# Two graph-attention layers on one core: node groups placed between the last sums, shorter last blocks, skip products at other slots

## The chip, the cores and the metric

One core of a Trainium2 chip runs the whole program. The metric is device time in microseconds (us), from the first to the last instruction with what lies around them. The engines are PE (TensorE), DVE (VectorE), ACT (ScalarE), POOL (GpSimd) and SP (which here only starts DMAs). Each runs its own queue in order, and the queues meet through semaphores.

## What is computed

3125 nodes with 128 features, 50000 edges sorted by destination, two layers of attention with two heads, a residual and a layer norm:

```python
def _transformer_conv(x, src, dst, qw, qb, kw, kb, vw, vb, sw, sb):
    q = (x @ qw + qb).reshape(N, H, D); k = ...; v = ...
    alpha = jnp.einsum('ehd,ehd->eh', q[dst], k[src]) * scale
    m = jax.ops.segment_max(alpha, dst, num_segments=N)
    ex = jnp.exp(alpha - m[dst])
    denom = jax.ops.segment_sum(ex, dst, num_segments=N)
    w = ex / (denom[dst] + 1e-16)
    agg = jax.ops.segment_sum(w[:, :, None] * v[src], dst, num_segments=N)
    return agg.mean(axis=1) + x @ sw + sb
h = _transformer_conv(x, src, dst, q1_w, ...) + x @ lin1_w + lin1_b
out = _transformer_conv(h, src, dst, q2_w, ...) + h @ lin2_w + lin2_b
x = _layernorm(x + out)
```

## The kernel before

**Chunks and bins.** The sorted edges are cut into chunks of 128, with a step for each pair of chunk and bin of 128 nodes: 416 steps (`STEPS`) for 391 chunks and 25 bins. I call a step, too, a chunk. The steps are grouped in blocks (`SIZES`); a block is what one scan of maxima covers.

**A layer.** For each step POOL gathers the 128 source rows by an indirect DMA (L407) into one of 98 ring places of `gathered`. PE spreads q k^T of the destination bin to the edges (`step_t`, L667, three products), and DVE multiplies it with the gathered rows and adds up (`step_alpha`, L930), which gives alpha. When a block has its alphas, `scan` runs over nine slots: PE transposes (L688 to L709), ACT copies (L477 to L485), and DVE does the segmented maxima both ways (L971 to L1010). Then each chunk of the block is weighed: DVE (`far_apart`, L941) or ACT (L492) marks which edge belongs to which node, ACT makes exp of it (`weigh`, L508, one for each head), PE multiplies with the gathered rows into a PSUM bank (`step_u`, L679), and DVE adds the bank to the bin's sums (`step_add`, L961). Three banks take turns.

**The order.** It is written by hand. `slots()` gives for each slot t the step whose alpha is made, the piece of a scan, and the chunks that are weighed; all four engines walk the same list. The chunks of a block are spread evenly over the slots of the next block, from nine slots after its end (`S_SLOTS`); the last block has `TAIL_SLOTS` = 24 slots. In slots without a step of alpha DVE makes all the marks, in the others every sixth (`DVE_EVERY`).

**The end of a layer.** Within the tail, every third slot from slot 421 on, PE makes a group of skip products x @ (s + lin) (`make_skip`, L655) into bank 0 or 1, and DVE copies it into `skip` (L950, layer 0) or adds it to `x_rows` (L953, layer 1). After the last sum come seven node groups of up to four bins (G = 4, the last has one bin). Group g: DVE normalises the sums (`normalise`, L1072 to L1074), PE transposes them (L747, L751), ACT copies ratio and head 0 (L541, L542), and head 1 is copied by DVE in layer 0 (L1086) and by ACT in layer 1 (L544). PE projects with v's weights (bias L762, products L767) into `bank_p`, of which there are two. DVE adds the skip rows (L1095 or L1100). In layer 0 PE transposes the result (L778), ACT copies it into `xT` (L549), and SP stores it to `h_d` (L356), from which layer 1 gathers; POOL waits for all seven stores (L400). In layer 1 DVE makes the statistics (L1105 to L1116), ACT the root (L553) and the normalised rows (L558), and SP stores them (L362, L366).

On each engine the loop over g does, in one turn, the newest step of group g and the later steps of groups g-1, g-2 and g-3. Here is the order of one turn on PE: transposes of group g; projection of group g-1; in layer 0 the transposes of group g-2's result.

## Time and profile before

| | before |
|---|---|
| median of three runs | 1239.3 us (1238.72 to 1239.43) |
| span of the profiled execution | 1238.0 us |
| PE busy | 993.4 us, 80% |
| DVE busy | 983.5 us, 79% |
| ACT busy | 784.5 us, 63% |
| POOL busy | 801.5 us, 65% |
| mean granted PE clock | 0.940 of 2.4 GHz |

The busy shares are means over stages that differ. POOL is busy at one level through both layers and idle between them and at the end, as the slices of the page show. So the two stretches after the last gather of a layer are read apart from the rest. In the rows of a timeline the columns are start, duration, engine, line, operation, out<-in, count, and in brackets the idle time before it with what ended it. PEld is PE's weight load, which starts a product.

### The profile page before, as it was taken

Reading aid. Unit: us, or ns where it says so; the run is one execution under the profiler, and the core shown is the slowest. Engines: PE = TensorE matmul, PEld = TensorE weight load, DVE = VectorE, ACT = ScalarE, POOL = GpSimd, SP = SyncE. Lnnn points to the kernel's source line nnn. Section 1 sums busy time; section 2 is a strip of 40 time slices with the busy share of each in tenths; the row PEclk is TensorE's granted clock in tenths of the full one; section 3 lists DMA queues with packets and bytes.
Section 4 is the critical chain, followed back from the end, with each engine's and each line's share of the span. In section 5 each row is a group of like instructions: output and inputs, shape, how many; then the busy total and the mean of one; then the engine's idle time right before and its main releaser. Section 6 shows DMA issues by size and latency. Waiting matters only on the chain.

```text
span 1238.0 us, 30556 instructions
## 1 busy us (share of the span) xinstructions
PE 993.4 (80%) x6796; PEld 791.4 (64%) x6796; DVE 983.5 (79%) x5252; ACT 784.5 (63%) x2594; POOL 801.5 (65%) x854
## 2 busy tenths in 40 slices
PE   4868987878877878789896776978886878888887
PEld 2647766766666667678653655757675757667775
DVE  4799986878787878889567687878787887879876
ACT  0456866676676768677254564758575768678655
POOL 3777777777777777750057777777777777777100
PEclk9989999899999999999797999999899999999888
DMA  4223332222222222210032222222232323222001
GB/s 112 88 77 89 89 84 80 78 80 80 78 81 80 78 82 84 73 42 1 27 102 79 79 80 77 80 80 78 80 87 71 89 73 85 77 80 63 17 2 52
DMA packets 53531, 90.21 MB, mean 73 GB/s; under 512 B 17499, under 2 KB 25969, under 8 KB 53361
## 3 DMA queue, kind: packets, MB, share of 16 engines
q0 software_dynamic: 26624, 54.58, 16.4%
q1 hardware_dynamic: 24145, 32.62, 8.7%
q8 instruction: 67, 1.10, 0.4%
q10 hardware_dynamic: 2592, 1.07, 0.3%
q14 instruction: 103, 0.84, 0.2%
HBM read 84.86 MB, written 3.34 MB: 71 GB/s over the span
## 4 chain that ended last, share of the span: by engine, by line
DMA 28%; PE 21%; POOL 20%; issue 15%; DVE 13%; ACT 2%; DVEq 1%; SPq 0%; POOLq 0%; ACTq 0%
POOL gathered L407 20%; DMA gathered<-h_rows,src_e 14%; DMA gathered<-in_x,src_e 14%; PE ps L679 9%; PE ps L667 5%; DVE acc L961 4%; DVE junk L930 3%; PE ps L767 2%; PE ps L751 1%; PE ps L762 1%; ACT whot L508 1%; DVE max_b L999 1%; DVE apart L941 1%; DVE max_f L997 1%; PE ps L655 0%
## 5 line engine op out<-in xcount | busy, mean ns | idle before, releaser
L508 ACT ACTIVATE whot<-apart,below 128x128 f32<-128x128 bf16 x1664 | 550.3, 388 | 139.7 <-DVE apart L941 127.5
L679 PE MATMUL ps<-gathered,whot 128*128 128x129 f32 x3328 | 566.1, 297 | 62.4 <-ACT whot L508 44.0
L930 DVE SCALAR_TENSOR_TENSOR junk<-ps,gathered 128x129 f32<-128x129 f32 x1664 | 413.0, 286 | 163.6 <-issue 113.8
L667 PE MATMUL ps<-table,hot_t 128*128 x2496 | 445.7, 287 | 101.8 <-DVE junk L930 80.5
L679 PEld LDWEIGHTS ps<-gathered,whot 128*128 128x128 f32 x3328 | 457.1, 200 | 100.0 <-DVE acc L961 64.7
L407 POOL DMA_INDIRECT gathered<-in_x,src_e x416 | 399.8, 961 | 144.3 <-issue 68.0
L407 POOL DMA_INDIRECT gathered<-h_rows,src_e x416 | 397.5, 955 | 126.6 <-issue 62.2
L667 PEld LDWEIGHTS ps<-table,hot_t 128*128 128x128 bf16 x2496 | 249.3, 100 | 212.3 <-issue 157.3
L961 DVE TENSOR_TENSOR acc<-ps,acc 128x258 f32 x832 | 350.2, 421 | 14.9 <-PE ps L679 5.4
L492 ACT ACTIVATE apart<-col_b,ndl_e 128x128 bf16<-128x128 bf16 x618 | 239.2, 387 | 0.0
L930 DVE DVE_READ_ACCUMULATOR junk<-ps,gathered 128x1 f32 x1664 | 134.9, 81 | 0.4
L477 ACT COPY a_row<-ps 48x256 f32<-48x256 f32 (+5 forms) x20 | 7.3, 365 | 89.2 <-PE ps L688 89.2
L941 DVE TENSOR_SCALAR apart<-ncol_b,ndl_e 128x128 bf16<-128x128 bf16 x214 | 54.9, 256 | 0.0
L400 POOL MEMSET gathered<- 128x98 f32 x1 | 0.3, 271 | 80.0 <-DMA h_rows<-table 80.0
L920 DVE TENSOR_SCALAR hot_t<-dl_bc,part_f 128x1024 bf16<-128x1024 bf16 x104 | 51.7, 497 | 0.1
L481 ACT ACTIVATE shrink<-drop 2x1 f32<-2x1 f32 x20 | 4.0, 202 | 52.9 <-DVE drop L988 52.9
L485 ACT COPY below<-ps 128x96 f32<-128x96 f32 (+5 forms) x20 | 4.6, 228 | 52.1 <-PE ps L709 52.1
L644 PE MATMUL ps<-qk,xT 128*128 128x258 f32 x100 | 33.7, 423 | 0.6 <-ACT xT L549 0.6
L767 PEld LDWEIGHTS ps<-wv,gathered 128*128 128x128 f32 x200 | 26.6, 214 | 10.8 <-issue 10.6
L471 ACT CAST table<-left 128x258 bf16<-128x258 f32 x50 | 20.4, 408 | 15.0 <-DVE left L865 13.3
L767 PE MATMUL ps<-wv,gathered 128*128 128x128 f32 x200 | 29.5, 306 | 0.0
L865 DVE TENSOR_TENSOR left<-ps,table 128x258 f32<-128x258 f32 x50 | 21.0, 421 | 8.0 <-ACT table L468 4.3
(165 smaller groups left out, 561.0 us busy)
## 6 DMA issues: line engine op xcount, KB each, us to landing
dl_bc<-local_dst_rows SPq DMA_DIRECT2D x104, 256.0 KB
gathered<-in_x,src_e POOLq DMA_INDIRECT x416
gathered<-h_rows,src_e POOLq DMA_INDIRECT x416
h_rows<-table SPq DMA_DIRECT2D x6, 256.0 KB, 2.3
out<-x_rows SPq DMA_DIRECT2D x6, 256.0 KB
table<-in_L_gnn_q_w ACTq DMA_DIRECT2D x2, 128.0 KB
table<-in_L_gnn_k_w ACTq DMA_DIRECT2D x2, 128.0 KB
wv<-in_L_gnn_v_w ACTq DMA_DIRECT2D x2, 128.0 KB
```

The source lines that it names most:

```text
L407: nc.gpsimd.indirect_dma_start(out=gathered[:, t % RING, 0:F], out_offset=None, in_=rows[:, :], in_offset=bass.IndirectOffsetOnAxis(ap=src ...
L492: nc.scalar.activation(apart[:, c % UN, :], col_b[:, :], ACT.Square, bias=ndl_e[:, c:c + 1]).then_inc(S["apart_act"], 1)
L508: last = nc.scalar.activation(whot[:, c % UN, h, :], apart[:, c % UN, :], ACT.Exp, scale=FAR, bias=below[:, j % 2, h, o:o + 1])
L644: nc.tensor.matmul(bank_u[n % NB][:, 0:CW], xT[:, k * P:(k + 1) * P], qk[:, l, :], start=True, stop=False)
L667: last = nc.tensor.matmul(bank_t[n % NB][:, 0:CW], hot_t[:, n // BC % 2, t % BC, :], table[:, bass.ds(b, 1), part, :].rearrange("p o c -> ...
L679: last = nc.tensor.matmul(bank_u[n % NB][:, h * C1:(h + 1) * C1], whot[:, c % UN, h, :], gathered[:, c % RING, :], start=True, stop=True)
L767: last = nc.tensor.matmul(o, uT[q % 2][:, h, t * P:(t + 1) * P], wv[:, l, h * F:(h + 1) * F], start=False, stop=(t == k - 1 and h == HEADS ...
L865: V.tensor_tensor(left[:, n % 2, :], bank_u[n % NB][:, 0:CW], table[:, k, 0, :], ALU.subtract).then_inc(S["left_ready"], 1)
L920: V.tensor_scalar(hot_t[:, q % 2, :, :].rearrange("p k e -> p (k e)"), dl_bc[:, q % 2, :], part_f[:, 0:1], None, ALU.is_equal).then_inc(S[ ...
L930: last = V.scalar_tensor_tensor(out=junk[:, t % 2, h, :], in0=bank_t[n % NB][:, h * C1:(h + 1) * C1], scalar=1.0, in1=gathered[:, t % RING ...
L941: V.tensor_scalar(apart[:, c % UN, :], ncol_b[:, :], ndl_e[:, c:c + 1], None, ALU.not_equal).then_inc(S["apart_dve"], 1)
L961: V.tensor_tensor(bin_acc, bank_u[n % NB][:, 0:CW], bin_acc, ALU.add).then_inc(S["u_added"], 1)
```

## The change

Sizes of the blocks are 26, 36, 44, five of 48, then 42, 18 and 10: eleven blocks, not ten. The last block has 10 slots. There are 435 slots instead of 449, and then five more for the node groups. The node groups are placed by `norm_at`: group g is normalised in the first slot by which its last sum is added, slot 424 at the earliest, one group a slot; `node(l, g)` follows in the next. This gives normalise at slots 424, 425, 426, 427, 429, 433, 435 and node(0 to 6) at 425, 426, 427, 428, 430, 434, 436. Chunks 406 to 415 are weighed in slots 425 to 434, one a slot. The sums use two banks from chunk 388 on (`TWO_BANKS`), and the projection has one bank, bank 6, which is also that of the scans' rows and of the skip products. A skip group is made at slot 12 after the end of blocks 1 to 7. Its product goes in layer 0 into `x_rows` in the place of x, so x is loaded again in layer 1. The stores of h stand on SP's queue behind the first two loads of `dl_bc` of layer 1.

```diff
-SIZES = (26, 36, 44) + 4 * (48,) + (44, 40, 34)
+SIZES = (26, 36, 44) + 5 * (48,) + (42, 18, 10)
+TWO_BANKS = STARTS[-3]
-TAIL_SLOTS = 24
+TAIL_SLOTS = SIZES[-1]
-SKIP_SLOT, SKIP_EVERY = 5, 3
+SKIP_BLOCK, SKIP_SLOT = 1, 3
+SPARE = 24, 72
...
-        skip = tmp([BINS, F])
...
-        tmp = lender(gathered[:, :, :].rearrange("p s c -> p (s c)"))
+        tmp = lender(gathered[:, SPARE[0]:SPARE[1], :].rearrange("p s c -> p (s c)"))
...
-        bank_p = [ps[:, 3, :], ps[:, 4, :]]
+        bank_p = ps[:, 6, :]
...
+        def u_bank(c):
+            return bank_u[c % NB] if c < TWO_BANKS else bank_u[c % 2]
         def skip_group(t, late):
-            g, rest = divmod(t - STEPS - SKIP_SLOT - late, SKIP_EVERY)
-            return g if rest == 0 and 0 <= g < NGR else None
+            for g in range(NGR):
+                if t == STARTS[SKIP_BLOCK + g + 1] + S_SLOTS + SKIP_SLOT + late:
+                    return g
+            return None
+        def last_step(g):
+            return min(CHUNKS - 1 + G * g + G - 1, STEPS - 1)
...
+            norm_at[g] = max(added_at[last_step(g)], STEPS + S_SLOTS - 1, norm_at[g - 1] + 1 if g else 0)
+        NODE_SLOTS = range(LAST_SLOT + 1, norm_at[NGR - 1] + 5)
+        def node_tick(t):
+            return [g for g in range(NGR) if norm_at[g] == t - 1] + [g for g in range(NGR, NGR + 3)
+                                                                     if norm_at[NGR - 1] + g - NGR + 2 == t]
...
@@ SP: as before, and @@
+            def store_h():
+                for g in range(NGR):
+                    t0, k, _ = group(g)
+                    sp.wait_ge(S["rows_read"], g + 1)
+                    sp.dma_start(h_d.rearrange("(t p) f -> p t f", p=P)[:, t0:t0 + k, :],
+                                 h_out[g % 2][:, 0:k, :]).then_inc(h_saved[g % 2], 16)
+                load_x(S["x_again"])
...
+                    if l == 1 and q == 2:
+                        store_h()
...
@@ ACT, PE: the body of the old loop over g is now node(l, g), and @@
+                    for g in node_tick(t):
+                        node(l, g)
+                for t in NODE_SLOTS:
+                    for g in node_tick(t):
+                        node(l, g)
...
@@ PE, make_skip @@
-                pe.wait_ge(S["alpha_ready"], (l + 1) * STEPS)
-                if g >= 2:
-                    pe.wait_ge(S["skip_read"], l * NGR + g - 1)
+                pe.wait_ge(S["below_ready"], l * NBLK + SKIP_BLOCK + g + 1)
...
@@ PE, step_u @@
-                if n >= NB:
-                    pe.wait_ge(S["u_added"], n - NB + 1)
+                if c in (TWO_BANKS, TWO_BANKS + 1):
+                    pe.wait_ge(S["u_added"], n)
+                elif c > TWO_BANKS:
+                    pe.wait_ge(S["u_added"], n - 1)
+                elif n >= NB:
+                    pe.wait_ge(S["u_added"], n - NB + 1 if c >= NB else n)
...
@@ PE, scan, piece 0 @@
+                    if j > SKIP_BLOCK:
+                        pe.wait_ge(S["skip_read"], l * NGR + min(j - SKIP_BLOCK, NGR))
...
@@ PE, node, before the projection of q = g - 1 @@
-                        if q >= 2:
-                            pe.wait_ge(S["rows_read"], m - 1)
+                    if q >= 1:
+                        pe.wait_ge(S["rows_read"], m)
...
@@ DVE, read_skip @@
-                    V.tensor_copy(skip[:, t0:t0 + k, :], product).then_inc(S["skip_read"], 1)
+                    V.tensor_copy(rows, product).then_inc(S["skip_read"], 1)
                 else:
-                    rows = x_rows[:, t0:t0 + k, :]
+                    if g == 0:
+                        dve.wait_ge(S["x_again"], 32)
                     V.tensor_tensor(rows, rows, product, ALU.add).then_inc(S["skip_read"], 1)
...
@@ DVE, normalise, and the loop @@
+                dve.wait_ge(S["u_added"], l * STEPS + last_step(g) + 1)
+                if g == 0:
+                    dve.wait_ge(S["skip_read"], (l + 1) * NGR)
...
+                    for g in range(NGR):
+                        if norm_at[g] == t:
+                            normalise(l, g)
+                    for g in node_tick(t):
+                        node(l, g)
                 step_add(l, STEPS - 1, b[UN - 1])
```

`node(l, g)` on DVE does, in this order: in layer 0 the copy of head 1 of group g; then the add of the skip rows of group g-2, which frees `bank_p`; in layer 1 that group's statistics and the reciprocal root of group g-3. On ACT: the copies of group g; in layer 0 the copy of group g-2's result into `xT`; in layer 1 the root of group g-2 and the normalised rows of group g-3.

## Rows read from the trace of the kernel before

**Rows 1.** Waits: engine, line, released by, us in total, times, longest.
```profile
POOL gathered L400 <- DMA h_rows<-table: 80.0, 1, 80.0
```
**Rows 2.** Timeline, the end of the gathers of layer 0 and the last alpha.
```profile
547.77 0.94 POOL L407 DMA_INDIRECT gathered<-in_x,src_e  x1 [0.30 <-issue]
...
551.39 0.29 DVE L930 SCALAR_TENSOR_TENSOR junk<-ps,gathered 128x129 f32<-128x129 f32 x1 [0.67 <-issue]
```
**Rows 3.** Timeline, DVE, first and tenth alpha of the slots of block 8's scan.
```profile
509.10 0.28 DVE L930 SCALAR_TENSOR_TENSOR junk<-ps,gathered 128x129 f32<-128x129 f32 x1
...
523.32 0.28 DVE L930 SCALAR_TENSOR_TENSOR junk<-ps,gathered 128x129 f32<-128x129 f32 x1
```
**Rows 4.** Windows, L679 alone: stretch, length, busy (count) of PE and PEld, clock, DMA.
```profile
525.08:551.39 26.31, 17.95 (x110) 14.09 (x108) 1.00 0.20 51
```
**Rows 5.** Timeline, the tail of layer 0 and the first two normalises.
```profile
565.86 0.48 DVE L1021 TENSOR_SCALAR acc<-acc,factor  x2
...
581.07 7.84 ACT L508 ACTIVATE whot<-apart,below 128x128 f32<-128x128 bf16 x26 [0.35 <-DVE apart L941]
...
581.90 7.83 PE L679 MATMUL ps<-gathered,whot 128*128 128x129 f32 x52
...
584.57 0.43 DVE L961 TENSOR_TENSOR acc<-ps,acc 128x258 f32 x1
584.91 0.24 DVE L941 TENSOR_SCALAR apart<-ncol_b,ndl_e 128x128 bf16<-128x128 bf16 x1
...
590.41 0.17 DVE L1072 TENSOR_SCALAR gathered<-acc 128x8 f32<-128x8 f32 x1
...
592.00 0.16 DVE L1072 TENSOR_SCALAR gathered<-acc 128x8 f32<-128x8 f32 x1
```
**Rows 6.** Timeline, a group of skip products and its copy.
```profile
568.81 1.06 PE L655 MATMUL ps<-wskip,xT 128*128 128x128 f32 x8
...
570.00 0.68 DVE L950 COPY table<-ps 128x512 f32<-128x512 f32 x1
```
**Rows 7.** Timeline, one turn of the node groups of layer 0.
```profile
612.68 0.09 PEld L747 LDWEIGHTS ps<-ident,gathered 128*8 128x8 f32 x1
...
613.86 0.29 PEld L762 LDWEIGHTS ps<-bias_rows,ratio 10*128 10x128 f32 x2 [0.17 <-issue]
...
613.97 0.69 DVE L1086 COPY gathered<-ps 128x512 f32<-128x512 f32 x1 [1.58 <-PE ps L751]
...
614.58 0.68 DVE L1095 TENSOR_TENSOR table<-table,ps 128x512 f32<-128x512 f32 x1
...
614.91 2.05 PE L767 MATMUL ps<-wv,gathered 128*128 128x128 f32 x16
...
617.13 0.09 PEld L747 LDWEIGHTS ps<-ident,gathered 128*8 128x8 f32 x1
...
617.44 0.58 ACT L549 COPY xT<-ps 128x512 f32<-128x512 f32 x1 [2.74 <-PE ps L778]
```
**Rows 8.** Timeline, POOL's restart for layer 1.
```profile
628.67 0.27 POOL L400 MEMSET gathered<- 128x98 f32 x1 [79.95 <-DMA h_rows<-table]
```
**Rows 9.** Timeline, layer 1: last gather, first normalise, a projection, the last rows.
```profile
1152.03 0.94 POOL L407 DMA_INDIRECT gathered<-h_rows,src_e  x1 [0.30 <-issue]
...
1194.61 0.17 DVE L1072 TENSOR_SCALAR gathered<-acc 128x8 f32<-128x8 f32 x1
...
1217.48 0.29 PEld L762 LDWEIGHTS ps<-bias_rows,ratio 10*128 10x128 f32 x2 [0.17 <-DVE x_rows L1100]
...
1230.40 0.28 DVE L1100 TENSOR_TENSOR x_rows<-x_rows,ps 128x128 f32<-128x128 f32 x1
```
**Rows 10.** Timeline, ACT before the first root.
```profile
1210.78 1.28 ACT L553 ACT_TABLE_LOAD   x1
```
**Rows 11.** Windows (columns: PE, PEld, DVE, ACT, POOL, clock) and a projection soon after.
```profile
592.00:596.00 4.00, 2.89 (x14) 2.55 (x15) 3.18 (x8) 0.73 (x2) 0.00 (x0) 0.50 0.00 0
...
599.20 3.78 PE L767 MATMUL ps<-wv,gathered 128*128 128x128 f32 x16
```

More of the change, by code:

```diff
@@ L782, in _ @@
+                    for g in node_tick(t):
+                        node(l, g)
+                for t in NODE_SLOTS:
+                    for g in node_tick(t):
+                        node(l, g)
         @block.vector
```

289 lines of the change are left out of this document (149 added, 140 removed).

## The prediction

> **What bounds the kernel now.** I read the waits first, then the timeline at the two ends of the gathers, then the stretches between. POOL issues one gather each 1.25 us (0.94 busy, 0.30 issue) [rows 2], 416 a layer, and nothing moves it from that pace: that is the bound of the steady part. Then it stands still for 80.0 us, until the last rows of h have landed [rows 1]. So a layer is a paced part, in which other engines have slack, and a part after the last gather (547.77, its sums' last step of alpha at 551.39 [rows 2]), in which PE, DVE and ACT set the time. That second part runs to POOL's restart at 628.67 [rows 8] and, in layer 1, from 1152.03 to the end [rows 9]. It has two pieces: the remaining sums, until the first normalise at 590.41 [rows 5] and 1194.61 [rows 9], and the node groups. Only a change of these pieces, twice, can move the span. I sum against the profiled span of 1238.0 us; the median run is 1239.3, so 1.3 is added at the end.
>
> **Prices.** PE: 52 products of sums in 7.83 us, so 0.60 a chunk [rows 5]. ACT: 26 weights in 7.84, so 0.30 an activation; a chunk costs two, and a third where ACT makes apart [rows 5]. DVE: a sum and the next apart start 0.34 apart, apart adds 0.24: 0.58 a chunk in the tail [rows 5]. Between 525.08 and 551.39 the schedule has 28 chunks and 23 steps of alpha (the row holds 110 products, 55 a head [rows 4]): 28 x 0.60 leaves 9.5, 0.41 of PE a step. PE was full there. A scan with its nine steps and ten chunks took 509.10 to 523.32, 14.2 us [rows 3]; DVE's own work there is 9 x 0.42 + 10 x 0.34 + about 6.4 of scan + 0.7, so DVE sets a scan stretch.
>
> **Skip products moved.** A group is 1.06 us of PE and 0.68 of DVE [rows 6]. Seven leave the tail of each layer. In the steady part a block of 48 slots lasts 60 us and needs about 49 of PE and 48 of DVE; 1 us more is caught up before the gathers end, so I cost it at nothing there (if the cover were gone: 7 us a layer). The waits it adds (PE for below_ready at slot 12 after a block, the next scan for skip_read) are for work done slots before.
>
> **x loaded twice.** On SP's queue it stands behind the h stores and ahead of the loads of dl_bc from the third on. Its reader is DVE at slot 75, some 90 us later. Zero; the upper bound is one late dl_bc, a few us, which the ring would absorb. The h stores now stand behind two loads of dl_bc whose buffers were free long before: zero.
>
> **Blocks.** Sizes 5 x 48, 42, 18, 10 for 4 x 48, 44, 40, 34. After the last step of alpha 27 chunks remain instead of 45, but the list of slots shows the price: slots 397 to 414 carry 42 chunks, 2.33 each, and one more scan is in them. Stage by stage, from slot 388 at 509.10 + 6 x 1.25 = 516.6 (gather pace):
> Slots 388 to 396, a scan with 11 chunks: 14.2 [rows 3], to 530.8.
> Slots 397 to 405, 21 chunks: ACT 60 activations x 0.30 = 17.9, PE 9 x 0.41 + 21 x 0.60 = 16.3, DVE 12. With handovers 18.4, to 549.2; the gathers would have allowed 11.3.
> Slots 406 to 414, 21 chunks and a scan: ACT 18.4, DVE 14.2 + 11 x 0.34 = 17.9, PE 17.3. Three full queues, 19, to 568.2.
> Slots 415 to 424: before, nine such slots with 11 chunks and two skip copies took 14.0 (551.8 to the rescale at 565.86 [rows 5]). Seven more chunks on DVE (+4.1), no skip copies (-1.2), one alpha (+0.4): 17.3, to 585.5.
> Two PSUM banks for the sums from chunk 388 on let a chunk pass in about 0.67 instead of 0.60: hidden by DVE here. So at 585.5 ten chunks are left and all skips are done; before, at that time, some nine chunks were left. The blocks gain next to nothing: the work was moved into slots that were full too. All gain must come from the node groups beginning 4.9 us earlier.
>
> **Node groups between the sums, layer 0.** PE's work from there is 10 x 0.60 + 6.25 groups x 4.45 (612.68 to 617.13 [rows 7]) = 33.8. But the queues run in order, and I followed them group by group:
> One bank_p. PE's projection of group g-1 now waits until DVE has read group g-2, and DVE reads it only behind its copy of group g's transposes. In the trace the copy begins at 613.97, the read at 614.58 for 0.68, while PE went on at 613.86 [rows 7]. So PE stands 1.35 us in each of five groups: 6.8.
> ACT's place. node(g) on ACT ends with the wait for h_tp and the copy of xT (0.58 [rows 7]); the weights of the next chunk stand behind it, and PE's chunk behind those: from the end of h's transposes to PE's next product 1.4, three times: 4.2.
> Start: normalise(0) 1.6 (590.41 to 592.00 [rows 5]) and the copies that transposes(1) needs: 1.7 + 1.8. Normalise(5), which waits for the sum of chunk 413: 1.5. Last groups' handovers 0.9. Store to restart 1.6.
> Sum 52.3: restart at 637.8, not 628.67: **+9.1**.
>
> **Layer 1.** The first normalise comes 36.8 after the last gather's issue, at 1189.8. PE: 6.0 + 6.25 x 4.0 = 31.0. Here ACT makes both copies and one bank_p costs little: at 1217.48 PE already goes on as DVE's read ends [rows 9]. What it meets instead is the root. Now one table load stands before the first root, 1.28 us [rows 10], and the exponentials are over by then. With roots at slots 427, 428, 430 and 434 and exponentials between them, ACT must load seven times instead of once. By my walk through the queues PE waits 1.8, 3.5 and 3.6 us for the weights of chunks 409, 410 and 412, behind copies, root, two loads and four normalised tiles. With start 3.0, normalise(5) 1.3, handovers 2.5 and the 7.6 from the last rows' add (1230.40) to the end [rows 9]: 31.0 + 8.9 + 14.4 = 54.3, end at 1244.1: **+6.1**.
> The page "ScalarE: Activation LUTs" of the Trainium skill (Table sets: the hidden batching unit) speaks against this: do all of one set, then the other, since exp then sqrt means two loads. By its 2.66 us a switch, drain included, six more would cost some 8 us more than the sum has; in the trace the root follows the load directly, so I keep 1.28.
>
> **Clock.** From 592 to 605 PE was granted 0.50, that is 1.2 GHz [rows 11], after it had stood while the first group was normalised; sixteen projections took 3.78 against 2.05 at 2.4 GHz [rows 11, 7]. That loss, about 5.5 us a layer, is in the time before. After the change no single long gap stands there, but PE is idle over 1 us twice a group. Bounds: nothing, or half speed for most of the phase (+3.3 a group). I take half of what was lost before, 2.7 a layer: +5.4.
> The page "TensorE: Matmul & The Clock Gate" (A second HAM failure mode: psum-queue depth-cycling) of the Trainium skill describes such short gaps between groups as making the clock swing; it is the clock rival below, and no stretch before has just this pattern.
>
> **Sum.** 1238.0 + 9.1 + 6.1 + 5.4 + 1.3 = 1259.9; I say 1259.
>
> **Rivals.**
> It works as meant (faster): PE stays filled, since chunks and groups cover each other's waits. Restart at 585.5 + 33.8 + 1.7 + 1.6 = 622.6, end 7.9 earlier by the same sum: 1225. For it: 38.3 us of node phase now hold 28 of PE work. It decides if PE's gap behind a group's transposes is under 0.3 us. Against: the copy stands first on DVE. 0.08.
> No change: the projection and ACT waits fall into each other, 11 us of them go: about 1240. 0.06.
> Root and exponential share a table after all: 6 x 1.28 less, 5 of them on the path: 1253. Against: the load before the first root. 0.08.
> The clock stays at 1.2 GHz for most of both node phases: 20 more, 1279. For it: PE's new gaps come in every group, where the one gap before was enough [rows 11]. 0.15.
> The forecast, own range 1250 to 1270: 0.63.
>
> **How the numbers follow.** The measurement tells about 0.2% from no change. Faster 0.09, within it 0.05, slower 0.86. From 1240 to 1279 leaves out the faster case, part of the even one and half of the clock's: 0.18. The largest unknown inside is the first normalise (580 to 590).
>
> **What would show it.** The last step of alpha comes near 568 instead of 551 with the gathers' end unchanged; the first normalise at 585 +- 4; PE waiting for DVE's add of rows 1.3 us a group in layer 0; seven table loads in the tail of layer 1 (eight in all, with the one at the start); skip products in the steady part without a later gather. I am wrong if alpha ends before 560, or if the node groups take under 45 us from the first normalise in layer 0.

## The result, and the profile after

| | before | after |
|---|---|---|
| median of four runs | 1239.01 us (1236.45 to 1239.43) | 1282.97 us (1279.99 to 1285.69) |
| ratio, 95% interval | | 1.036 [1.034, 1.038] |
| span of the profiled execution | 1238.0 us | 1281.6 us |
| mean granted PE clock | 0.940 | 0.917 |

The change makes the kernel 44 us slower, where 20 were forecast: the direction holds, the size doesn't. First the waits of the changed kernel (engine, line, released by, us in total, times, longest; L435 is POOL's restart, L723 the sums' products, L543 their weights, L1016 DVE's add, L563 the copy of `xT`, L785 the projection's bias, L1114 the add of the skip rows):

```profile
POOL gathered L435 <- DMA h_rows<-table: 101.3, 1, 101.3
...
PE ps L723 <- ACT whot L543: 63.2, 71, 3.4
...
DVE acc L1016 <- PE ps L723: 49.1, 50, 7.0
...
ACT xT L563 <- PE ps L801: 27.4, 7, 5.8
...
PE ps L785 <- DVE table L1114: 6.5, 5, 1.4
```

POOL stands 101.3 us where it stood 80.0 [rows 1]: 21.3 of the 43.6 us between the spans lie in this pause between the gathers of the two layers. Then the timeline, at the places of [rows 2, 5, 8, 9]:

```profile
517.40 0.29 DVE L983 SCALAR_TENSOR_TENSOR junk<-ps,gathered 128x129 f32<-128x129 f32 x1
...
548.07 0.95 POOL L442 DMA_INDIRECT gathered<-in_x,src_e  x1 [0.30 <-PE ps L723]
...
550.02 0.28 DVE L983 SCALAR_TENSOR_TENSOR junk<-ps,gathered 128x129 f32<-128x129 f32 x1
...
572.79 0.28 DVE L983 SCALAR_TENSOR_TENSOR junk<-ps,gathered 128x129 f32<-128x129 f32 x1
...
594.27 0.17 DVE L1092 TENSOR_SCALAR gathered<-acc 128x8 f32<-128x8 f32 x1
...
650.28 0.27 POOL L435 MEMSET gathered<- 128x98 f32 x1 [101.26 <-DMA h_rows<-table]
...
1175.49 0.95 POOL L442 DMA_INDIRECT gathered<-h_rows,src_e  x1 [0.30 <-issue]
...
1220.93 0.16 DVE L1092 TENSOR_SCALAR gathered<-acc 128x8 f32<-128x8 f32 x1
```

The steps of alpha are those of slots 388, 406 and 415. The last gather of layer 0 ends 0.3 us later. The first normalise comes at 594.27, 3.9 us *later* than before, though 27 chunks and not 45 were left behind the last alpha and ten of them stand behind it; and from there to the restart it is 56.0 us, where it was 38.3. In layer 1 the gathers take 524.9 us from first to last, against 523.0; the first normalise comes 44.5 us after the last gather's end, against 41.6; from it to the end it is 60.7, against 43.4.

What PE waits for in the node groups of layer 0:

```profile
606.41 1.12 PE L785 MATMUL ps<-bias_rows,ratio 10*128 10x512 f32 x2 [1.38 <-DVE table L1114]
...
611.31 0.68 PE L723 MATMUL ps<-gathered,whot 128*128 128x129 f32 x4 [1.36 <-ACT whot L543]
...
614.35 1.12 PE L785 MATMUL ps<-bias_rows,ratio 10*128 10x512 f32 x2 [1.38 <-DVE table L1114]
...
619.25 1.27 PE L723 MATMUL ps<-gathered,whot 128*128 128x129 f32 x8 [1.36 <-ACT whot L543]
...
622.87 1.12 PE L785 MATMUL ps<-bias_rows,ratio 10*128 10x512 f32 x2 [1.38 <-DVE table L1114]
...
629.40 2.67 PE L723 MATMUL ps<-gathered,whot 128*128 128x129 f32 x16 [1.36 <-ACT whot L543]
...
633.07 0.28 PE L770 MATMUL ps<-ident,gathered 128*8 128x128 f32 x1 [1.00 <-DVE gathered L1094]
...
635.60 1.12 PE L785 MATMUL ps<-bias_rows,ratio 10*128 10x512 f32 x2 [1.38 <-DVE table L1114]
...
642.02 1.12 PE L785 MATMUL ps<-bias_rows,ratio 10*128 10x512 f32 x2 [0.98 <-DVE table L1114]
```

Two waits alternate. PE waits 1.38 us ahead of a projection, because there is only one bank, and 1.36 ahead of a chunk's products, because of the place of the `xT` copy in ACT's queue. In layer 1 there are also the table loads on ACT (first the loads, then PE's waits for weights):

```profile
1253.81 1.28 ACT L567 ACT_TABLE_LOAD   x1
...
1255.11 0.21 ACT L567 ACTIVATE gathered<-gathered 128x4 f32<-128x4 f32 x1
...
1256.87 1.28 ACT L543 ACT_TABLE_LOAD   x1
...
1225.88 1.20 PE L723 MATMUL ps<-gathered,whot 128*128 128x129 f32 x4 [1.99 <-ACT whot L543]
...
1241.25 0.68 PE L723 MATMUL ps<-gathered,whot 128*128 128x129 f32 x4 [1.88 <-ACT whot L543]
...
1250.30 1.27 PE L723 MATMUL ps<-gathered,whot 128*128 128x129 f32 x8 [1.12 <-ACT whot L543]
...
1259.00 3.71 PE L723 MATMUL ps<-gathered,whot 128*128 128x129 f32 x16 [3.42 <-ACT whot L543]
```

The grouped lines count four loads at the root (L567) and three at the exponentials (L543) in this stretch. And this is a hole in the sums at slot 406, the first of the scan of the block of 18 (ACT, then DVE):

```profile
550.93 0.36 ACT L512 COPY a_row<-ps 18x256 f32<-18x256 f32 x1 [1.42 <-PE ps L734]
...
551.20 0.40 ACT L527 ACTIVATE apart<-col_b,ndl_e 128x128 bf16<-128x128 bf16 x1
...
551.51 0.68 ACT L543 ACTIVATE whot<-apart,below 128x128 f32<-128x128 bf16 x2
...
550.56 0.43 DVE L1016 TENSOR_TENSOR acc<-ps,acc 128x258 f32 x1
...
553.22 0.43 DVE L1016 TENSOR_TENSOR acc<-ps,acc 128x258 f32 x1 [2.24 <-PE ps L723]
```

ACT waits 1.42 us for PE's transposes of the new block's alphas (L734) while the next weights stand behind that copy; the sums then miss 2.24 us.

### The profile page after: what moved, and what is told of

The parts are those of the page before. It is cut to its first block, busy times and chain, and to the rows that moved or that the text cites. A ratio compares the mean times of both kernels' runs of the same rounds, so it can differ in the third digit from the quotient of the medians.

```text
span 1281.6 us, 30697 instructions
## 1 busy us (share of the span) xinstructions
PE 1014.7 (79%) x6824; PEld 809.9 (63%) x6824; DVE 989.4 (77%) x5268; ACT 801.3 (63%) x2636; POOL 804.4 (63%) x854
## 4 chain that ended last, share of the span: by engine, by line
PE 33%; issue 18%; DVE 15%; DMA 14%; POOL 13%; ACT 5%; DVEq 1%; SPq 0%; ACTq 0%; POOLq 0%
PE ps L723 17%; POOL gathered L442 13%; PE ps L707 10%; DMA gathered<-h_rows,src_e 7%; DMA gathered<-in_x,src_e 6%; DVE junk L983 5%; DVE acc L1016 4%; ACT whot L543 3%; PE ps L790 2%; PE ps L774 1%; DVE max_b L1054 1%; PE ps L785 1%; DVE max_f L1052 1%; PE ps L695 1%; DVE a_end L1026 1%
## 5 line engine op out<-in xcount | busy, mean ns | idle before, releaser
L723 PE MATMUL ps<-gathered,whot 128*128 128x129 f32 x3328 | 583.0, 304 | 79.6 <-ACT whot L543 63.2
L543 ACT ACTIVATE whot<-apart,below 128x128 f32<-128x128 bf16 x1664 | 553.7, 388 | 142.0 <-DVE apart L994 126.3
L723 PEld LDWEIGHTS ps<-gathered,whot 128*128 128x128 f32 x3328 | 472.7, 206 | 123.4 <-DVE acc L1016 70.8
L707 PE MATMUL ps<-table,hot_t 128*128 x2496 | 452.3, 291 | 107.6 <-DVE junk L983 86.3
L1016 DVE TENSOR_TENSOR acc<-ps,acc 128x258 f32 x832 | 349.9, 421 | 59.3 <-PE ps L723 49.1
L707 PEld LDWEIGHTS ps<-table,hot_t 128*128 128x128 bf16 x2496 | 253.2, 102 | 211.8 <-issue 157.3
L527 ACT ACTIVATE apart<-col_b,ndl_e 128x128 bf16<-128x128 bf16 x648 | 250.8, 387 | 0.0
L512 ACT COPY a_row<-ps 48x256 f32<-48x256 f32 (+6 forms) x22 | 8.0, 365 | 97.7 <-PE ps L734 97.7
L435 POOL MEMSET gathered<- 128x98 f32 x1 | 0.3, 273 | 101.3 <-DMA h_rows<-table 101.3
L994 DVE TENSOR_SCALAR apart<-ncol_b,ndl_e 128x128 bf16<-128x128 bf16 x184 | 46.4, 252 | 0.0
L516 ACT ACTIVATE shrink<-drop 2x1 f32<-2x1 f32 x22 | 4.5, 202 | 56.1 <-DVE drop L1043 56.1
L520 ACT COPY below<-ps 128x96 f32<-128x96 f32 (+6 forms) x22 | 4.9, 223 | 47.7 <-PE ps L755 47.5
L790 PE MATMUL ps<-wv,gathered 128*128 128x128 f32 x200 | 32.6, 327 | 0.0
L506 ACT CAST table<-left 128x258 bf16<-128x258 f32 x50 | 20.4, 407 | 16.4 <-DVE left L918 14.7
```

The source lines that it names most:

```text
L527: nc.scalar.activation(apart[:, c % UN, :], col_b[:, :], ACT.Square, bias=ndl_e[:, c:c + 1]).then_inc(S["apart_act"], 1)
L543: last = nc.scalar.activation(whot[:, c % UN, h, :], apart[:, c % UN, :], ACT.Exp, scale=FAR, bias=below[:, j % 2, h, o:o + 1])
L707: last = nc.tensor.matmul(bank_t[n % NB][:, 0:CW], hot_t[:, n // BC % 2, t % BC, :], table[:, bass.ds(b, 1), part, :].rearrange("p o c -> ...
L723: last = nc.tensor.matmul(u_bank(c)[:, h * C1:(h + 1) * C1], whot[:, c % UN, h, :], gathered[:, c % RING, :], start=True, stop=True)
L790: last = nc.tensor.matmul(o, uT[q % 2][:, h, t * P:(t + 1) * P], wv[:, l, h * F:(h + 1) * F], start=False, stop=(t == k - 1 and h == HEADS ...
L994: V.tensor_scalar(apart[:, c % UN, :], ncol_b[:, :], ndl_e[:, c:c + 1], None, ALU.not_equal).then_inc(S["apart_dve"], 1)
```

## The experiments

Five sets of two to four kernels, each beside the kernel before on its chip. **The chips differ**: in the first set the kernel before took 1237.6 us, as in the result; in the others, on four other chips, 1647.5, 1624.1, 1646.2 and 1640.3. So a kernel is compared with those of its own set, and between sets only by ratio. The ratios are the record's and can differ by 0.003 from the ratio of the two medians. One more view helps: how long a layer runs after its last gather is issued, split at the start of the reciprocal of the first normalise (the second instruction of that step). In layer 0 it ends with the first gather of layer 1, in layer 1 with the program. It is read from one profiled execution of each kernel:

| kernel, set | layer 0: to normalise, to restart | layer 1: to normalise, to end |
|---|---|---|
| before | 42.8, 38.4 | 42.8, 43.2 |
| after | 46.4, 56.1 | 45.6, 60.5 |
| e2_skip, 1 | 39.6, 37.2 | 39.1, 41.9 |
| e10_blocks_skip, 1 | 51.1, 37.2 | 48.7, 42.3 |
| e7_old_blocks, 1 | 28.2, 75.7 | 28.0, 79.3 |
| e3_rows_first, 1 | 48.6, 44.9 | 47.2, 60.3 |
| e4_three_banks, 2 | 86.8, 61.1 | 86.8, 62.3 |
| e5_roots_last, 2 | 89.2, 62.3 | 90.4, 50.9 |
| e6_xt_later, 2 | 92.3, 51.5 | 90.4, 64.2 |
| e8_all_fixed, 2 | 89.5, 46.0 | 89.3, 50.9 |
| after_again, 3 | 91.5, 56.3 | 91.3, 59.4 |
| e12_four_edits, 3 | 85.1, 48.0 | 87.8, 51.6 |
| e12_again, 4 | 88.2, 43.7 | 86.2, 48.4 |
| e10_again, 4 | 93.9, 37.2 | 94.2, 41.9 |
| e11_again, 4 | 92.1, 37.2 | 90.5, 42.3 |
| e13_five, 5 | 83.4, 43.7 | 83.8, 49.8 |
| e11_third, 5 | 91.2, 37.2 | 90.5, 43.5 |

### Set 1: the parts one by one

**e2_skip**: old blocks, node groups at the end with two projection banks, three sum banks throughout. Only the skip products, the second load of x and the place of the h stores are new. Against the changed kernel (the lines that carry the edit; `...` stands for lines left out):

```diff
-SIZES = (26, 36, 44) + 5 * (48,) + (42, 18, 10)
+SIZES = (26, 36, 44) + 4 * (48,) + (44, 40, 34)
-TWO_BANKS = STARTS[-3]
+TWO_BANKS = STEPS
-TAIL_SLOTS = SIZES[-1]
+TAIL_SLOTS = 24
...
-        bank_p = ps[:, 6, :]
+        bank_p = [ps[:, 3, :], ps[:, 4, :]]
...
-            norm_at[g] = max(added_at[last_step(g)], STEPS + S_SLOTS - 1, norm_at[g - 1] + 1 if g else 0)
+            norm_at[g] = LAST_SLOT + 1 + g
...
```

> The changed kernel with the old blocks (44, 40, 34, tail of 24 slots), all node groups behind the last sum, three banks for the sums and two for the projection: of the change only the skip products in the steady part, x loaded twice and the later place of the h stores are left. Theory (the skips are covered there): seven groups of 1.06 us of PE leave each tail, about 5 us a layer come back, less 2 us for a slower start of layer 1's gathers: 1239 - 8 = about 1231. Rival (the steady part has no room, each group delays alphas up to the end): 1239 or more.

1232.5 us (1231.4 to 1233.7), ratio 0.996 [0.994, 0.998]: below before by 0.4%, which is small but outside the interval, and 1.5 us above the 1231 of the theory. **e10_blocks_skip** is the same kernel with the new sizes.

> The same as the kernel with the skips moved alone, but with the new blocks (48, 42, 18, 10): the difference of the two is the blocks. In the changed kernel the first normalise came at 594.3 with ten chunks (6.7 us) left, so the last sum would be at 601, against about 585 with old blocks. Theory (slots 397 to 424 are full and one more scan stands in them): 10 to 16 us a layer more than the skips alone, 1251 to 1262. Rival (as my prediction had it, the blocks only move work, +-1 us a layer): within 3 us of the skips alone.

1254.1 us (1251.6 to 1256.4), ratio 1.013 [1.011, 1.016]. So the blocks alone cost 21.6 us, about half in each layer, as the theory had it; the forecast had them at nothing. In the table the time to the first normalise goes from 39.6 to 51.1 and from 39.1 to 48.7, and the node groups stay as they were. The time lies in the 18 slots ahead of the last alpha, which now carry 42 chunks.

**e7_old_blocks**: the changed kernel with the old sizes; node groups between the sums of a last block of 34 chunks.

```diff
-SIZES = (26, 36, 44) + 5 * (48,) + (42, 18, 10)
+SIZES = (26, 36, 44) + 4 * (48,) + (44, 40, 34)
-TAIL_SLOTS = SIZES[-1]
+TAIL_SLOTS = 24
```

> The changed kernel with the old blocks; the node groups still stand between the last sums (the first in the slot of chunk 394's sum). Together with the three others this closes a table of two by two. Theory (blocks and the placing of the groups both cost, and add up): 1283 less twice 10 to 16, 1250 to 1262; so 20 to 25 us more than the skips alone. Rival (placing the groups costs only in the crowded slots of the new blocks): below 1240.

1285.4 us (1283.0 to 1285.9), ratio 1.038 [1.036, 1.040]. All that was expected is missed: I had priced the interleaving as the same whatever the blocks. With the old blocks it costs 53 us (1285.4 against 1232.5), with the new 29 (1283.0 against 1254.1), perhaps because 22 chunks and not ten then stand among the groups, each with its waits; that was not tested. And the old sizes move something else with them: `TWO_BANKS = STARTS[-3]` is then chunk 342 and no longer 388, so the sums have two banks for 74 chunks of a layer and not for 28. How much of the 53 is that, no run tells. The two parts of the change don't add.

**e3_rows_first**: in layer 0 DVE adds the rows of group g-2 and only then makes the copy of group g's transposes; six lines change place.

```diff
             def node(l, g):
-                if l == 0 and g < NGR:
-                    ... V.tensor_copy(uT[g % 2][:, 1, 0:w], bank_h1[:, 0:w]).then_inc(S["uT1_ready"], 1)
                 if 2 <= g < NGR + 2:
                     ...
+                if l == 0 and g < NGR:
+                    ... V.tensor_copy(uT[g % 2][:, 1, 0:w], bank_h1[:, 0:w]).then_inc(S["uT1_ready"], 1)
```

> The changed kernel with one edit on DVE: in layer 0 the add that reads the projection's bank stands ahead of the copy of the next group's transposes. Theory (PE waits 1.35 us a group for that add, because of the one bank): five groups, 1283 - 6.8 = 1276, all of it in layer 0 between the first normalise and the restart of the gathers (56.0 to about 49). Rival (the wait for ACT's copies or for the weights ends last anyway): less than 2 us.

1275.4 us (1270.1 to 1278.2), ratio 1.030 [1.026, 1.033], 7.6 us less than the changed kernel of the result. In layer 0 the wait of the bias for DVE's add goes from 6.5 us to 0.3; the other 1.2 stood in layer 1 already and stay:

```profile
PE ps L785 <- DVE x_rows L1113: 1.2, 2, 0.8
...
PE ps L785 <- DVE table L1108: 0.3, 1, 0.3
```

```profile
611.65 0.68 PE L723 MATMUL ps<-gathered,whot 128*128 128x129 f32 x4 [1.36 <-ACT whot L543]
...
618.14 1.27 PE L723 MATMUL ps<-gathered,whot 128*128 128x129 f32 x8 [1.35 <-ACT whot L543]
...
625.22 2.68 PE L723 MATMUL ps<-gathered,whot 128*128 128x129 f32 x16 [1.35 <-ACT whot L543]
```

The 1.36 of ACT stand untouched. The cause of the term "one bank_p, 6.8" is shown. The 7.6 us aren't its size alone: by the table layer 0's node groups take 11.2 us less, and 2.2 and 1.6 come back ahead of the first normalises. Of the 11.2, PE's idle time is 5.8 and its busy time 5.5, for it was granted the full clock here and 0.88 in the changed kernel (window from the first normalise to the restart; length, then PE, PEld, DVE, ACT, POOL busy, clock, DMA):

```profile
596.10:641.10 45.00, 35.50 (x237) 27.31 (x238) 24.06 (x57) 13.78 (x39) 0.27 (x1) 1.00 0.13 38
```

### Set 2: the other orders, one by one

**e4_three_banks**: chunk 388 is weighed in slot 415, so the changed kernel has two banks from slot 415 on, and this one from chunk 406, slot 425.

```diff
-TWO_BANKS = STARTS[-3]
+TWO_BANKS = STARTS[-2]
```

> The changed kernel, but the sums keep three banks up to slot 406 + 9 = 415 instead of 406, that is, two banks are used only in the last block. Theory (two banks tie sum and add together: DVE's add waited 5.0 us on PE and PE 4.5 us on DVE's add between 574 and 594 us, against 1.6 and 0.9 in the kernel with the new blocks and the nodes at the end): nothing in slots 406 to 414, where the stage was as long with three banks, and little in the last block, which still has two: 1281 to 1285, a ratio to the kernel before of 1.034 to 1.038. Rival (two banks from 406 on are what made the stage 406 to 414 take 22.8 us and not 19): both layers get back 3 to 4 us: about 1275, 1.030.

**e5_roots_last**: in layer 1 all roots and what follows them from node(6) on.

```diff
-                if l == 1 and 2 <= g < NGR + 2:
-                    t0, k, _ = group(g - 2)
+                for q in late(l, g, 2):      # from g = 6 on, first 0 to 4 at once
+                    t0, k, _ = group(q)
... and so for late(l, g, 3), on ACT the normalised rows, on DVE the reciprocal roots
```

> The changed kernel, but in layer 1 the square roots, reciprocals and normalised rows of the groups begin only at the seventh group step, so that the exponentials of the remaining slots come before all roots and ScalarE changes its table once and not seven times. Theory (each change back costs PE its wait of 1.1 to 3.4 us on the next weights, less 0.7 as usual: 1.9, 2.0, 1.1 and 3.4 us are the four waits): 5 to 8 us less, all in layer 1: 1275 to 1278, a ratio of 1.029 to 1.032. Rival (the loads lie beside matmuls at half clock anyway): 1281 to 1283.

**e6_xt_later**: ACT's copy of h's transposes at the head of the next turn.

```diff
             def node(l, g):
+                if l == 0 and 3 <= g < NGR + 3:
+                    q = g - 3 ...
+                    nc.scalar.copy(xT[:, t0 * P:t0 * P + w], bank_b[:, 0:w]).then_inc(S["hT_ready"], 1)
                 if g < NGR:
                     ...
-                if l == 0 and 2 <= g < NGR + 2:
-                    q = g - 2 ...
-                    nc.scalar.copy(xT[:, t0 * P:t0 * P + w], bank_b[:, 0:w]).then_inc(S["hT_ready"], 1)
```

> The changed kernel, but ScalarE's copy of the transposed h of a group stands one group step later, at its head, when the transposes have long been made. Theory (in layer 0 the weights behind that copy come late and PE waits 1.36 to 1.38 us on them, six times, of which about half would be waited for the node transposes anyway): 4 to 6 us less in layer 0, nothing in layer 1: 1277 to 1279, a ratio of 1.031 to 1.033. Rival (PE's clock and its sequence set the node phase, the wait only moves): 1281 to 1283.

**e8_all_fixed**: e3, e5 and e6 together.

> The changed kernel with three edits together: VectorE adds the projected rows ahead of its copy in layer 0 (7.6 us by a run), roots last (5 to 8) and ScalarE's copy a step later (4 to 6). If they add: 1283 - 7.6 - 6.5 - 5 = 1264, a ratio of 1.020. If what remains is PE's own work at a low clock, the second and third give back little: 1272 to 1275. Either way it stays above the kernel with the new blocks and the nodes at the end (1254): what remains between them is not orders and table loads but work on PE between its sums.

Medians 1692.5, 1691.9, 1692.6 and 1671.2 beside 1647.5; ratios 1.025 [1.022, 1.028], 1.025 [1.022, 1.029], 1.025 [1.022, 1.029] and 1.012 [1.008, 1.016]. The absolute expectations are void on this chip, and the changed kernel itself was not in the set. By its ratios on two other chips, 1.036 and 1.033, each single edit takes off 0.8 to 1.1%; by the medians alone it is 0.3 to 0.9%. Within the set, e8 lies 20.8 us below e5, which lacks rows first and the later copy, and 21.4 below e6, which lacks rows first and the late roots. With 7.6 for rows first, that leaves 13 to 14 for either of the other two. Its 1.012 is below the 1.020 that was expected if the edits add. Whether it stays above the kernel with the new blocks and the nodes at the end is open across chips: that one has 1.013 on the first chip and, in set 4, 1.007.

The traces tell what kind of time it is. PE's idle time, its busy time and its granted clock, from the reciprocal of the first normalise to the restart or to the end:

| kernel | layer 0: idle, busy, clock | layer 1: idle, busy, clock |
|---|---|---|
| after | 15.3, 40.9, 0.88 | 19.7, 40.8, 0.78 |
| after_again | 15.3, 41.0, 0.88 | 19.6, 39.7, 0.81 |
| e3 (rows first) | 9.5, 35.4, 1.00 | 19.2, 41.0, 0.79 |
| e4 (three banks) | 16.6, 44.5, 0.83 | 20.2, 42.1, 0.76 |
| e5 (roots last) | 15.8, 46.4, 0.80 | 16.5, 34.4, 0.86 |
| e6 (copy later) | 12.0, 39.5, 0.90 | 18.7, 45.5, 0.70 |
| e8 (all three) | 5.6, 40.4, 0.85 | 16.5, 34.4, 0.86 |
| e12_four_edits | 6.3, 41.7, 0.82 | 17.2, 34.4, 0.86 |
| e12_again | 6.3, 37.4, 0.92 | 17.2, 31.2, 0.90 |
| e13_five | 6.3, 37.4, 0.92 | 17.2, 32.6, 0.90 |

The idle time hardly changes between traces of the same order. The busy time does: e12 is one kernel, run on two chips, and its layer 0 differs by 4.3 us, all of it busy time at another clock. So a difference of a few us between two single traces isn't yet the edit's.
Roots last: 50.9 us from the first normalise to the end, against 62.3 and 64.2 in the set; 5 to 8 were expected. Over all traces here, the five with the roots last take 48.4 to 51.6 and the five with the roots between 59.4 to 64.2: **about 11 us** between the means. Only 3 of it is idle time (19.7 to 16.5). The rest is PE's busy time: every one of the five with the roots last has a clock of 0.86 to 0.90 there, every one of the others 0.70 to 0.81. One table load is left in that stretch.
Copy later: 51.5 us to the restart, against 61.1 and 62.3 in the set, but against only 56.1 and 56.3 in the two traces of the changed kernel: **5 to 11 us**, where 4 to 6 were expected. The idle time falls by 3.3 to 4.6, which is the forecast's 4.2; the rest goes with a clock of 0.90 against 0.80 to 0.88, and e12 shows that the clock of this stretch moves by 0.10 without an edit. What is left on PE:

```profile
852.32 1.28 PE L723 MATMUL ps<-gathered,whot 128*128 128x129 f32 x8 [0.25 <-DVE acc L1016]
...
854.60 0.28 PE L770 MATMUL ps<-ident,gathered 128*8 128x128 f32 x1 [1.00 <-DVE gathered L1094]
...
857.13 1.83 PE L785 MATMUL ps<-bias_rows,ratio 10*128 10x512 f32 x2 [1.38 <-DVE table L1114]
```

Three banks: 86.8 us to the first normalise in both layers; the six numbers of the kernels of the set without that edit have a mean of 90.2. **About 3.4 us a layer**, and the traces of sets 3 and 4 agree: 85.1 to 88.2 with three banks (e12_four_edits, e12_again), 91.5 and 91.3 without (after_again). The theory said little, the rival 3 to 4: the rival has the size, but not the place. It laid the time on slots 406 to 414, and there the changed kernel has three banks itself. The time lies behind slot 415, where the theory saw no room: from its alpha to the reciprocal in layer 0, e4 takes 18.3 us, e5 20.4 and after_again 22.8.

### Sets 3 to 5: the sum of the edits, and the start of a block

**e12_four_edits** (e8 with three banks) and **after_again** (the changed kernel as it is):

> The changed kernel with four edits together: VectorE's add of the projected rows ahead of its copy in layer 0, ScalarE's copy of the transposed h a group step later, roots and normalised rows of layer 1 only from the seventh group step on, and three sum banks up to the last block. By the traces of the runs with one or three of these edits (time from the last gather to the restart of layer 1, and from the last gather of layer 1 to the end): rows first 7 to 8 in layer 0; copy later 7 to 8 in layer 0; roots last 11 to 13 in layer 1; three banks 3.4 in each layer. If they add on the changed kernel: 1283 - 7.6 - 7.6 - 12 - 6.8 = 1249, a ratio to the kernel before of 1.008. Rival (PE's clock and its longer queue set what remains, orders only move waits): 1262 or more, 1.019.

> The changed kernel once more, unchanged, to stand beside the others of this set on one chip: 1283, a ratio to the kernel before of 1.036. If the three runs with one edit each, all at 1692 beside 1647 for the kernel before, brought nothing, the absolute distance to before is 44 there and here; if they brought what their traces show, this kernel stands further from before on such a chip: about 50 to 55.

1646.9 and 1673.7 beside 1624.1: ratios 1.014 [1.010, 1.017] and 1.033 [1.031, 1.036]. The edits together take 26.8 us off. The sum of the pieces was 34, which would have given 1.008; the rival had 1.019, and the measured value lies between. Either the edits share some of their effect, or the pieces, read from single traces, were taken too large. The changed kernel's distance to before, 49.6, lies just under what was expected from working edits (50 to 55), and 4.5 to 5.2 above that of the three single edits in set 2. **e12_again**, set 4:

> The changed kernel with the four edits (rows first, copy a step later, roots last, three banks up to the last block). On the other chip it was 26.8 us under the changed kernel beside it, where the sum of the single edits by their traces was 34. If the edits add in the same measure here: 1283 - 27 = 1256, a ratio of 1.014; if a chip with faster gathers shows them in full, 1249, 1.008.

1663.7 beside 1646.2, ratio 1.011 [1.009, 1.012], again between the two that were expected. Neither chip was of the first kind, so what the four bring there was not measured.

**e11_blocks_behind** and **b1_skip_behind** are e10 and e2 with one move in ACT's list, the copy of a block's row behind the weights of its slot:

```diff
-                    if s is not None:
+                    if s is not None and s[-1]:
                         scan(l, *s)
                     for c in cs:
                         ...
                         weigh(l, c)
+                    if s is not None and not s[-1]:
+                        scan(l, *s)
```

> The kernel with only the skip products moved, x loaded twice and the stores behind (old blocks, nodes at the end, 1232.5 measured), and in ScalarE's list the copy of a block's row of scores (the first piece of its scan) stands behind the weights of the slot and not ahead of them. Theory (ScalarE stood 1.4 us at that copy on PE's row transposes at each block's first slot while the weights of the slot were ready to be made): 11 blocks a layer, but only where ScalarE is what the sums wait for, in the drain: 0 to 3 us less: about 1231. Rival (the copy then comes later, and with it the maximum, the below row and the block's first weight): 0 to 4 more.

> The kernel with the new blocks, skips moved and the nodes at the end (1254.1 measured), with the same move of ScalarE's row copy behind the weights of its slot. Theory (of the 3.8 us by which slots 406 to 414 took longer than reckoned, the 3.5 us hole in the sums at the first slot of the short block comes from that wait in ScalarE's order): about 2 us less in each layer: 1250, a ratio of 1.010. Rival (the hole is the row transposes and the copy themselves, whatever their order): 1254.

1614.1, ratio 0.993 [0.991, 0.996], and 1628.0, ratio 1.003 [1.001, 1.006], where 0.996 and 1.013 stood for the kernels without the move on the first chip. The first is what the theory had, the second is below its 1.010. Set 4 holds the pair on one chip:

> The kernel with the new blocks, the skips moved and the nodes at the end, unchanged, as the yardstick for the next run on its chip. On a chip of the first set's kind 1254, a ratio of 1.013; on one of the kind of the second and third set the same distance of 16 us to before if the blocks cost the same there, 4 to 6 if the gathers' later landing covers part of what they cost.

> The same kernel with ScalarE's row copy behind the weights of its slot. Theory (ScalarE stood 92 us in all, 22 times, on the row transposes at that copy, 16.9 of it in the last five blocks of layer 0, and the 3.5 us hole in the sums at the first slot of the short block comes from it): 4 to 10 us under the kernel of the run beside it. Rival (the hole only moves): within 1.5 us of it.

> The kernel with only the skips moved, old blocks, nodes at the end, and ScalarE's row copy behind the weights of its slot: without the last edit it took 1232.5, a ratio of 0.9958. Theory: 2 to 6 us less, a ratio of 0.991 to 0.994. Rival: 0.996 or more.

e10_again 1657.3, 1.007 [1.005, 1.010]: 11.1 us above before, neither the 16 nor the 4 to 6. e11_again 1646.8, 1.000 [0.998, 1.002], and b1_again 1633.8, 0.992 [0.991, 0.994], as the theories had them. The move is worth 10.4 us there with the new blocks; with the old ones no pair stands on one chip. How much of it lies after the last gather the timelines tell, first without the move (set 4), then with it (e11_third, set 5):

```profile
763.45 0.43 DVE L1016 TENSOR_TENSOR acc<-ps,acc 128x258 f32 x1
...
766.12 0.43 DVE L1016 TENSOR_TENSOR acc<-ps,acc 128x258 f32 x1 [2.24 <-PE ps L723]
...
763.82 0.36 ACT L512 COPY a_row<-ps 18x256 f32<-18x256 f32 x1 [1.42 <-PE ps L734]
...
786.74 0.36 ACT L512 COPY a_row<-ps 10x256 f32<-10x256 f32 x1 [2.16 <-PE ps L734]
```

```profile
765.12 0.43 DVE L1018 TENSOR_TENSOR acc<-ps,acc 128x258 f32 x1
...
766.12 0.43 DVE L1018 TENSOR_TENSOR acc<-ps,acc 128x258 f32 x1 [0.57 <-PE ps L725]
...
765.73 0.34 ACT L512 COPY a_row<-ps 18x256 f32<-18x256 f32 x1
...
786.75 0.36 ACT L512 COPY a_row<-ps 10x256 f32<-10x256 f32 x1 [0.24 <-PE ps L736]
```

Between two adds 2.67 us become 1.00, and the ten slots from one copy to the next 22.9 become 21.0: 1.9 us. From the alpha of slot 406 to that of slot 415 it is 22.75 without the move and 21.09 in the three traces of e11, which has it. The first two waits of e10_again are the same to the hundredth as in the changed kernel on the first chip (1.42, 2.24), so the slow gathers play no part in them. The table shows more: from the last gather to the first normalise 93.9 and 94.2 become 91.2 to 92.1 and 90.5, that is 5.5 to 6.4 us in the two layers together. The rest of the 10.4 is not placed; the waits at block starts earlier in the layer might carry it, and no run tests that.

**e13_five** (e12 with that move) and **e11_third**:

> The changed kernel with the four edits (rows first, copy a step later, roots last, three banks up to the last block) and also ScalarE's row copy behind the weights of its slot. Theory: that last edit brought 10 us without the steps between the sums (1646.8 beside 1657.3) and brings as much here: a ratio to before of 1.003 to 1.005. If the steps between the sums were worth their overlap once the orders are mended, it would come out under the kernel of the run beside it; what the sets so far say is that it stays 5 to 8 us above it. Rival (with groups between the sums the order at the block's start no longer matters): 1.010.

> The kernel with the new blocks, skips moved, nodes at the end and the row copy behind the weights, beside the run above. On a chip where the gathers land as in the trace of before: 1244 to 1250, a ratio of 1.005 to 1.010, if the edit is worth 2 to 5 us per layer in the drain alone; 1254, 1.013, if the whole of its 10 us lay in waits that slow gathers make. On one where they land later: 1.000.

1645.6 (1635.2 to 1649.3), 1.003 [1.000, 1.006], and 1647.6, 1.004 [1.002, 1.007]. The 1.003 is as expected; the second lies between the values given for the two kinds of chip. With all orders mended the groups between the sums cost nothing more than at the end, and bring nothing. The expected 5 to 8 us between them are missed.

The best kernel of the study is e2's with ACT's move: 0.993 and 0.992 on two chips. Without the move, 0.996 on the first. Both lie below the kernel before by more than their intervals, though by less than 1%, and neither has the blocks or the groups between the sums.

## Why the forecast was wrong

**The sums' end was priced too low: +8.8 us in layer 0, +7.7 in layer 1.** The forecast had the first normalise 36.8 us after the last gather (it says its issue; by its 1189.8 it counts from the end, 0.94 later). Measured are 45.2 and 44.5; in layer 0 the gather itself ends 0.3 later. Stage by stage in layer 0: slot 388 at 517.40 for 516.6 and slot 406 at 550.02 for 549.2, so up to there only 0.8 of start. Then "three full queues, 19" took 22.8, and "17.3, to 585.5" took 21.5.
Slots 406 to 414: the step that failed is the sum of queues' work without the order in them. It took the longest of ACT 18.4, DVE 17.9 and PE 17.3 and 0.6 for handovers, but at the slot where a scan begins ACT waits in order, with the weights behind. Shown: 1.7 to 1.9 of the 3.8 us. The other 2 stay open.
Slots 415 to 424: the step "two banks ... hidden by DVE here" failed; no row stood behind its 0.67 us a chunk either. With the nodes at the end and three banks, e10_blocks_skip took 18.8 from the alpha of slot 415 (573.24) to the rescale (592.02), against 21.5 in the changed kernel, and by e4 a layer gets back about 3.4 us. So 2.7 to 3.4 of the 4.2 us are the two banks, and about 1 stays open. The windows show that the clock falls too (PE, PEld, DVE, ACT, POOL busy, clock, DMA), the changed kernel first, e10_blocks_skip behind it:

```profile
574.00:594.30 20.30, 16.02 (x83) 13.40 (x81) 14.84 (x57) 12.14 (x39) 0.00 (x0) 0.75 0.00 0
```

```profile
574.00:592.00 18.00, 14.11 (x86) 11.77 (x84) 15.81 (x60) 13.21 (x44) 0.00 (x0) 0.91 0.00 0
```

PE was granted 0.75 against 0.91. How much of the 3.4 is the bank itself and how much the clock was not told apart.

**The clock in the node groups: about 5.5 us in layer 0, and more in layer 1, for 2.7 each.** It can be read from PE's busy time. In layer 0 the same PE instructions were busy 35.4 us in e3, at full clock, and 40.9 in the changed kernel, at 0.88. In layer 1 they were busy 40.8 at 0.78, and 31.2 in e12_again at 0.90. Here are the windows of the changed kernel, layer 0 and layer 1:

```profile
594.30:650.30 56.00, 40.93 (x236) 31.85 (x236) 23.87 (x57) 13.62 (x38) 0.02 (x1) 0.89 0.10 30
1221.00:1281.60 60.60, 40.94 (x211) 31.54 (x211) 31.17 (x120) 33.47 (x78) 0.00 (x0) 0.78 0.09 27
```

In e12_again PE was busy for about the 31.0 of the sum, so its work itself was not priced too low there. The rival in which PE stays at 1.2 GHz for most of both phases is out: the means are 0.89 and 0.78 (before: 0.82 and 0.79). But the clock took about 10 us more than the forecast had, half of the rival's 20.

**Node groups of layer 0: the waits right, the total by some luck.** 52.3 and 2.7 for the clock were forecast, 56.0 measured. The waits that the walk through the queues gave, 1.35 in each of five groups and 1.4 three times, are there as 1.38 (four times, and a 0.98) and 1.36 (three times), and the edits took them away: 5.8 and 3.3 us of idle time one by one, 9.7 together, for 6.8 and 4.2 forecast. But the terms as they are listed add up to 53.9 and not to 52.3; the 1.6 from store to restart is missing from the sum. And in the total two misses cancel: PE was idle for 15.3 us where the sum leaves 18.5 beside PE's work, and busy for 40.9 where it has 36.5 with the clock.

**Node groups of layer 1: 3.7 us too low.** 57.0 were forecast, 60.7 measured. Seven loads came as counted, and the PE waits of 1.8, 3.5 and 3.6 as 1.88, 1.12 and 3.42, with one of 1.99 ahead of them. The waits weren't the step that failed: PE was idle for 19.7 us, where the sum has 23.3 beside PE's work. It was busy for 40.8, where 31.0 and 2.7 for the clock stood. So the term that was too small is the clock's, by 7 us. The sixteen products behind the 3.42 took 3.71 us (1259.00), where sixteen in layer 0 took 2.67 (629.40); the granted clock was 0.56 in the one stretch and 1.00 in the other. That the low clock goes with the roots between the exponentials is shown by the ten traces above; which of the gaps brings it is not. The page "ScalarE: Activation LUTs" (What ACT_TABLE_LOAD costs) of the Trainium skill puts a switch at 2.66 us with its drain. Here a load takes 1.28 and the root starts at once behind it (1253.81, 1255.11). What six loads more cost the layer, about 11 us, is neither number: about 3 are idle time of PE, the rest its lower clock.

**The gathers of layer 1: 1.9 us.** They were forecast to take no longer. e2_skip and e10_blocks_skip show 1.5 and 0.7 in the same view (524.4 and 523.7 against 523.0, first gather to last). It is near the limit of what one execution tells, and no run takes the second load of x away; open.

The misses are 8.8 + 1.0 in layer 0 and 1.9 + 7.7 + 3.7 in layer 1, 23.1 of the 23.0 between 1258.6 and the span of 1281.6.

**Skips moved**: no cost and a gain of 5.1 us where the rest stays as it was. **"The blocks gain next to nothing"** was too kind by 21.6 us, measured with the groups at the end, and that is where most of the miss begins: the same two stretches of slots carry it.

## What to carry to other kernels

Where a bounded stretch meets a full one, work moved from behind the last input to ahead of it is only moved if the slots in front have room on every engine, and in each engine's order. Price a full stretch by a walk through the queues, not by the sum of the fullest: the walk found the waits of layer 0's groups within 0.04 us for all but one, the sum was 8 us off in the stage where it was used. Split a stretch of a trace into idle and busy time of the engine that sets it, with the clock beside them, before a difference is put down to an order. And when phases are interleaved, every instruction that waits for the one phase delays the other behind it: add first and copy then, put a copy one turn later, keep the roots behind the last exponential, or nothing is gained.

## What the runs showed of the hardware

The granted clock of TensorE isn't fixed for a kernel: e12, the same program on two chips, was granted 0.82 and 0.92 over the node groups of layer 0, with PE idle for 6.5 us in both windows and busy for 41.7 and 37.4 us.

```profile
800.80:849.00 48.20, 41.69 (x237) 33.24 (x238) 24.33 (x57) 13.80 (x39) 0.27 (x1) 0.82 0.12 35
```

```profile
813.60:857.50 43.90, 37.38 (x237) 30.01 (x238) 24.35 (x57) 13.79 (x39) 0.27 (x1) 0.92 0.13 38
```

The same kernel took 1238 us on one chip and 1624 to 1648 on four others. There the waits have releasers that the profile cannot name; this is the changed kernel on the chip of set 3, at the start of layer 0, with POOL issuing gathers each 1.25 us all the while:

```profile
82.43 0.58 ACT L489 COPY xT<-ps 128x512 f32<-128x512 f32 x1 [10.62 <-remote]
```

On the first chip the seven copies of this line start within some 4 us. Here ACT waits 10.6 us ahead of a copy, and they come in steps of 11.2, the time in which POOL issues nine gathers. What holds the engines there is not settled. Two things follow for measuring: edits worth some 10 us behind the last gather are best read from that part of the trace, and the move of ACT's copy brought 10 us there of which some 6 lie behind the last gathers; its worth on the first kind of chip was not measured.
